# Row sums sent round by DMA, and V's high and low halves in one stationary tile, in a gated first layer followed by two attentions and a feed-forward part

## The reference

```python
def attention(x, ctx, Wq, Wk, Wv, Wo, bo):
    q, k, v = ...                                    # split in 16 heads of 64
    sim = jnp.einsum('bihd,bjhd->bhij', q, k) * SCALE
    attn = jax.nn.softmax(sim, axis=-1)
    out = jnp.einsum('bhij,bjhd->bihd', attn, v).reshape(b, n, HEADS * D_HEAD)
    return out @ Wo + bo
h = layernorm(x, ln1_g, ln1_b)
x = attention(h, h, a1_Wq, a1_Wk, a1_Wv, a1_Wo, a1_bo) + x          # 256 keys
h = layernorm(x, ln2_g, ln2_b)
x = attention(h, context, a2_Wq, a2_Wk, a2_Wv, a2_Wo, a2_bo) + x    # 120 keys
h = layernorm(x, ln3_g, ln3_b)
u, gate = jnp.split(h @ ff_Wp + ff_bp, 2, axis=-1)
x = u * jax.nn.gelu(gate, approximate=False) @ ff_Wo + ff_bo + x
```

## Time and profile before

| what | value |
|---|---|
| median of three executions (lowest, highest) | 1032.53 us (1032.07, 1035.41) |
| profiled execution: own time, span | 1037.63 us, 1035.8 us |
| TensorE matmuls busy | 997.8 us, 96% |
| VectorE busy | 709.0 us, 68% |
| ScalarE busy | 623.9 us, 60% |
| GpSimd busy | 365.7 us, 35% (16 memsets of V's zero columns: 2.4) |
| mean granted TensorE clock | 0.990 |
| chain of work that ended last | PE 81%, DVE 9%, ACT 7%, issue 2%, POOL 1% |

### The profile page before, as it was taken

The page is one execution under the profiler, slowest core; times in us unless marked ns, Lnnn a source line. Parts: engine busy times, 40 slices in busy tenths (PEclk is TensorE's granted clock), DMA queues, the critical chain, the costliest instruction groups (busy, mean ns, idle before and its releaser), DMA issues.

```text
span 1035.8 us, 21731 instructions
## 1 busy us (share of the span) xinstructions
PE 997.8 (96%) x8044; PEld 938.7 (91%) x8044; DVE 709.0 (68%) x1594; ACT 623.9 (60%) x1945; POOL 365.7 (35%) x515
## 2 busy tenths in 40 slices
PE   9899998999999999999999999999999998899998
PEld 9788777899999999999999989999999997899998
DVE  3476868867676767676768776677677667567674
ACT  2566646856565656565667666676676676434343
POOL 1021445533333333333333245455455454401010
PEclk9999999999999999999999989999999998999999
DMA  6220200103000000000003000300000001000110
GB/s 206 81 72 1 77 21 31 32 2 102 2 22 1 22 1 22 2 21 2 22 1 87 22 26 2 107 26 26 3 26 27 2 22 62 22 22 27 36 32 21
DMA packets 30446, 34.63 MB, mean 33 GB/s; under 512 B 4360, under 2 KB 23816, under 8 KB 30344
## 3 DMA queue, kind: packets, MB, share of 16 engines
q1 hardware_dynamic: 30344, 33.26, 10.5%
HBM read 24.86 MB, written 8.39 MB: 32 GB/s over the span
## 4 chain that ended last, share of the span: by engine, by line
PE 81%; DVE 9%; ACT 7%; issue 2%; POOL 1%; DVEq 0%; POOLq 0%
PE bank L1388 14%; PE bank L1390 14%; PE bank L1389 14%; PE bank L1650 8%; PE bank L1629 5%; PE bank L1412 5%; PE bank L1692 3%; PE bank L1694 3%; PE bank L1693 3%; PE bank L1666 3%; ACT p L771 2%; PE bank L1396 1%; PE bank L1519 1%; PE bank L1520 1%; PE bank L1521 1%
## 5 line engine op out<-in xcount | busy, mean ns | idle before, releaser
L578 POOL TENSOR_TENSOR oT_hi<-oT,ones 128x256 fp32r<-128x256 f32 x128 | 93.9, 733 | 364.2 <-DVE oT L1184 364.2
L771 ACT ACTIVATE p<-bank,negmax 128x256 f32<-128x256 f32 (+1 forms) x512 | 207.7, 427 | 20.8 <-DVE negmax L1161 16.0
L781 ACT CAST pT_hi<-bank 128x512 fp32r<-128x512 f32 (+1 forms) x256 | 110.8, 486 | 164.6 <-PE bank L1650 164.4
L1388 PE MATMUL bank<-hT_hi,w_hi 128*128 128x256 f32 x640 | 188.4, 294 | 4.9 <-DVE qkT_lo L1215 1.6
L1390 PE MATMUL bank<-hT_hi,w_lo 128*128 128x256 f32 x640 | 179.2, 280 | 0.0
L1389 PE MATMUL bank<-hT_lo,w_hi 128*128 128x256 f32 x640 | 179.0, 280 | 0.0
L1176 DVE TENSOR_TENSOR pT_lo<-bank,pT_hi 128x512 fp32r<-128x512 f32 (+1 forms) x256 | 129.6, 548 | 0.4
L1388 PEld LDWEIGHTS bank<-hT_hi,w_hi 128*128 128x128 f32 x640 | 121.6, 190 | 8.2 <-issue 4.7
L1157 DVE TENSOR_REDUCE negmax<-bank 128x2 f32<-128x512 f32 x128 | 82.2, 684 | 66.9 <-PE bank L1629 66.9
L1389 PEld LDWEIGHTS bank<-hT_lo,w_hi 128*128 128x128 f32 x640 | 121.3, 189 | 0.0
L1390 PEld LDWEIGHTS bank<-hT_hi,w_lo 128*128 128x128 f32 x640 | 120.9, 189 | 0.0
(11 more groups left out here) (207 smaller groups left out, 2773.4 us busy)
## 6 DMA issues: line engine op xcount, KB each, us to landing
w_stage<-in_weights SPq DMA_DIRECT2D x47, 256.0 KB, 4.0
x_in<-x_dram SPq DMA_DIRECT2D x24, 256.0 KB, 2.9
x_dram<-x_out SPq DMA_DIRECT2D x16, 256.0 KB, 3.2
l_x<-in_x SPq DMA_DIRECT2D x4, 512.0 KB, 5.3
x_dram<-l_out SPq DMA_DIRECT2D x4, 512.0 KB, 2.8
out_dram<-x_out SPq DMA_DIRECT2D x8, 256.0 KB, 3.2
w_stage<-in_weights SPq DMA_DIRECT2D x9, 128.0 KB, 4.4
l_ctx<-in_ctx SPq DMA_DIRECT2D x4, 180.0 KB, 4.6
```

Of the source, the lines that this page charges most:

```text
L578: nc.gpsimd.tensor_tensor(oh[:, G % PAIRS, :], of[:, :], ones[:, :], ALU.mult).then_inc(y["o_hi"], 1)
L771: last = nc.scalar.activation(p[:, G % 2, e, t * cols:(t + 1) * cols], scores_at(G, e, t), ACT.Exp, bias=negmax[:, G % 2, t, e:e + 1], acc ...
L781: nc.scalar.copy(pTh[0:r, G % 2, e, 0:n], bank[4 + e][0:r, 0:n]).then_inc(y["pT_hi"], 1)
L1388: nc.tensor.matmul(dst, lh, rh, start=(i == 0), stop=False)
```

## The change

The widened and transposed row sums are gone. The reciprocals of a pair go by DMA: `send_sums` writes them to DRAM as two rows of 256, one for each head, and `spread_sums` reads each row back to 64 partitions of `rsumT`, which has four buffers (`DEEP`). GpSimd multiplies, in `split_o`. V has one tile, in which each head has 128 columns, high and low side by side, and both halves of the transposed exponentials are multiplied by all 128. So low x low is summed too. The low values of a head come out on the other 64 partitions; ScalarE copies them across and VectorE adds. In cross-attention the head products alternate between banks 6 and 2, the scores between 0 and 1, and the transposed exponentials of both heads of a pair share one bank (4 or 5 in turn), with one copy and one subtraction for a pair. SP's list becomes a loop over the 128 steps with the loads, stores and weight units placed in it.

```diff
-VW = 3 * DH
+VW = 2 * DH
+DEEP = 4
...
+            def send_sums(G):
+                sp.wait_ge(y["rsum"], G + 1)
+                if G >= DEEP:
+                    sp.wait_ge(*spread_until(G - DEEP))
+                sp.dma_start(sums_dram[G % DEEP, :, :].rearrange("e (q t) -> q e t", t=NT),
+                             rs[:, G % 2, :].rearrange("q (e t) -> q e t", e=2)).then_inc(y[f"rsum_row{G % 2}"], 16)
+            def spread_sums(G):
+                sp.wait_ge(y[f"rsum_row{G % 2}"], 16 * (G // 2 + 1))
+                if G >= 2:
+                    sp.wait_ge(*spread_until(G - 2))
+                if G >= DEEP:
+                    sp.wait_ge(y["o_norm"], G - DEEP + 1)
+                for e in range(2):
+                    sp.dma_start(rT[e * DH:(e + 1) * DH, G % DEEP, :],
+                                 sums_dram[G % DEEP, e:e + 1, :].partition_broadcast(DH)).then_inc(y[f"rT{G % 2}"], 16)
...
-            for b in range(3 * B):
-                if b + 3 < 3 * B:
-                    load(b + 3)
-                store(b)
...
+            for G in range(STEPS):
+                b, i = divmod(G, PAIRS)
+                send_sums(G)
+                if G >= 1:
+                    spread_sums(G - 1)
...
+                if i == 3 and b >= 1:
+                    store(b - 1)
+                if i == 4:
+                    load(b + 2)
+                if i == 5 and B < b + 2 < 2 * B:
+                    load_context(b + 2)
+                if b == 1 and i < 4:
+                    load_weights(sp, 12 + i, 13 + i)
...
+                if b == 2 * B - 1 and i >= 6:
+                    load_weights(sp, 18 + i, 19 + i)
...
-            def widen_sums(G):
...
             def split_o(G):
+                pool.wait_ge(y["o_sum"], G + 1)
+                pool.wait_ge(*spread_until(G))
...
+                nc.gpsimd.tensor_tensor(on[:, :].rearrange("p (t q) -> p t q", t=NT),
+                                        of[:, G % DEEP, :].rearrange("p (t q) -> p t q", t=NT),
+                                        rT[:, G % DEEP, :].rearrange("p (q t) -> p t q", t=NT),
+                                        ALU.mult).then_inc(y["o_norm"], 1)
...
-            def copy_rT(G):
+            def copy_low_values(G):
                 act.wait_ge(y["o"], G + 1)
-                nc.scalar.copy(rT[:, :], bank[6][:, S:2 * S]).then_inc(y["rT_copied"], 1)
+                if G >= 2:
+                    act.wait_ge(y["o_sum"], G - 1)
+                nc.scalar.copy(ob[0:DH, G % 2, :], o_bank(G)[DH:128, 0:S])
+                nc.scalar.copy(ob[DH:128, G % 2, :], o_bank(G)[0:DH, S:2 * S]).then_inc(y["o_low"], 1)
...
             def inverse_sums(G):
                 dve.wait_ge(y["exp"], 2 * G + 2)
+                if G >= 2:
+                    dve.wait_ge(y[f"rsum_row{G % 2}"], 16 * (G // 2))
...
-            def normalise_o(G):
+            def add_low_values(G):
+                dve.wait_ge(y["o_low"], G + 1)
+                if G >= DEEP:
+                    dve.wait_ge(y["o_norm"], G - DEEP + 1)
+                nc.vector.tensor_tensor(of[0:DH, G % DEEP, :], o_bank(G)[0:DH, 0:S], ob[0:DH, G % 2, :], ALU.add)
+                nc.vector.tensor_tensor(of[DH:128, G % DEEP, :], o_bank(G)[DH:128, S:2 * S], ob[DH:128, G % 2, :],
+                                        ALU.add).then_inc(y["o_sum"], 1)
...
             def transpose_p(G):
...
+                else:
+                    pe.wait_ge(y["pT_lo"], 2 * G - 1 if G == STEPS // 2 else 2 * G - 2)
+                    for e in range(2):
+                        pe.wait_ge(y["exp"], 2 * G + e + 1)
+                        for t in range(NT):
+                            last = nc.tensor.transpose(pT_both(G)[:, e, t * 128:(t + 1) * 128],
+                                                       p[:, G % 2, e, t * SC:(t + 1) * SC], ident[:, :])
+                    last.then_inc(y["pT"], 2)
             def weighted_values(G):
...
+                    pe.wait_ge(y["o_sum"], G if G < STEPS // 2 else G - 1)
...
+                for e in range(2):
+                    dst = o_bank(G)[:, e * S:(e + 1) * S]
+                    for j in range(tiles):
+                        vs = vv[0:r, j, (2 * g + e) * VW:(2 * g + e + 1) * VW]
+                        pc = slice(j * S, (j + 1) * S)
+                        nc.tensor.matmul(dst, vs, pTh[0:r, G % 2, e, pc], start=(j == 0), stop=False)
+                        last = nc.tensor.matmul(dst, vs, pTl[0:r, G % 2, e, pc], start=False, stop=(j == tiles - 1))
```

More of the change, by code:

```diff
@@ L280, in build, with spread_until @@
         LAST = NI - 1
+        sums_dram = nc.dram_tensor("rsums_dram", (DEEP, 2, S), F32, kind="Internal").ap()
+        def spread_until(G):
+            return y[f"rT{G % 2}"], 32 * (G // 2 + 1)
         def out_banks(it):
@@ L338, in v_src, with v_dst @@
             return v_bank(b, c)[0:v_rows(b), :].rearrange("p (g e d) -> p g e d", g=4, e=2)
-        def v_dst(buf, b, c):
-            half = slice(c % 2 * 4 * VW, (c % 2 + 1) * 4 * VW)
-            return buf[0:v_rows(b), c // 2, half].rearrange("p (g s d) -> p g s d", g=4, s=3)[:, :, 0:3:2, :]
+        def v_dst(b, c, low):
+            part = vv[0:v_rows(b), c // 2, c % 2 * 4 * 2 * VW:(c % 2 + 1) * 4 * 2 * VW]
+            part = part.rearrange("p (g s d) -> p g s d", g=4, s=4)
+            return part[:, :, 1:3, :] if low else part[:, :, 0:4:3, :]
         def first_c():
@@ L380, in score_bank, with o_bank, pT_both @@
         def score_bank(G, e):
-            return bank[(2 * G + e) % 3 if G < STEPS // 2 else G % 3]
+            return bank[(2 * G + e) % 3 if G < STEPS // 2 else G % 2]
+        def o_bank(G):
+            return bank[6 if G < STEPS // 2 or G % 2 else 2]
+        def pT_both(G):
+            return bank[4 + G % 2][0:SC, :].rearrange("p (e n) -> p e n", e=2)
         def scores_at(G, e, t):
@@ L545, in first_layer @@
                     add_bias(0)
-                    pool.wait_ge(z["rps"], KT * NI)
-                    for v_ in (vh, vl):
-                        for pr in range(PAIRS):
-                            last = nc.gpsimd.memset(v_[:, :, pr * VW + DH:pr * VW + 2 * DH].bitcast(F32), 0.0)
-                    last.then_inc(zeros_ready, 1)
                 if it >= 1:
@@ L1174, in pT_low @@
[L1174 to L1184 removed]
+                if cols_of(G) == S:
+                    for e in range(2):
+                        dve.wait_ge(y["pT_hi"], 2 * G + e + 1)
+                        nc.vector.tensor_tensor(pTl[:, G % 2, e, :], bank[4 + e][:, :],
+                                                pTh[:, G % 2, e, :].bitcast(F32),
+                                                ALU.subtract).then_inc(y["pT_lo"], 1)
+                else:
+                    dve.wait_ge(y["pT_hi"], 2 * G + 2)
+                    nc.vector.tensor_tensor(pTl[0:SC, G % 2, :, 0:S], pT_both(G),
+                                            pTh[0:SC, G % 2, :, 0:S].bitcast(F32),
+                                            ALU.subtract).then_inc(y["pT_lo"], 2)
```

148 lines of the change are left out of this document (65 added, 83 removed).

## The result

The changed kernel takes 1043.14 us (median of six runs, 1038.82 to 1044.64) against 1033.97 for the kernel before on the same chip: a ratio of 1.0066, 95% interval 1.0034 to 1.0098. I had forecast 999. The profiled execution took 1038.82 us, its span is 1037.0.

| stage | before | after | change | forecast | full width | upper half first | short chain |
|---|---|---|---|---|---|---|---|
| self-attention | 412.3 | 381.9 | -30.4 | -38 | 375.0 | 378.6 | 383.9 |
| cross-attention to step 127 | 296.4 | 324.2 | +27.8 | -4 + 8.6 | 294.1 | 311.9 | 287.9 |
| from step 127 on | 153.0 | 157.0 | +4.0 | 0 | 156.6 | 155.9 | 157.2 |

The account below looks back on a forecast made before the run. TensorE was taken to bound self-attention, a VectorE and ScalarE hand-over chain cross-attention. From 1032.5 us: -38 self-attention, -4 cross-attention, +8.6 clock falls, sum -33.4, giving 999 us; range 976 to 1015.

Parts of the forecast that it names:

- -38: Self-attention: TensorE stays the bound and loses transposes and products, six middle batches 32.4 us, first 3.5, last 2.
- -4 + 8.6: Cross-attention: 4 us saved by the batches, 8.6 us lost to two new falls of TensorE's clock.
- a chain that TensorE's savings don't shorten: Cross-attention: batches run on VectorE and ScalarE handing over to each other; a middle batch saves 0.6 us, not 4.9.
- rival 4: Row sums' DMA round trip limits the steps, from landings of 5.2 us on; slower than before, 1100 us at 6.0; chance 0.04.
- rival 5: VectorE becomes the bound in self-attention too, half of the 38 us stays away: 1018 us; chance 0.06.
- Rival 1: TensorE is the bound in cross-attention too, the chain has slack: 957 us, or 973 for half; chance 0.16.
- A second one started right behind the first adds less than its duration: Split copy and addition per pair: second instruction overlaps the first, adding 0.33 us on VectorE and 0.27 on ScalarE.
- 4.2 and 5.1: Cross-attention from i = 2 on: distances in us between successive maxima on VectorE, today 3.87 and 4.77.
- The clock: Cross-attention: a 2.8 us TensorE wait at i = 4 brings two falls to 1.2 GHz, 4.3 us each, +8.6.
- rival 3: Cross-attention: the clock falls in six or seven batches, +28 us instead of +8.6, 1018 us; chance 0.10.
- 0 to +2: Start of the feed-forward part: last pair's output about 1.3 us later, last weight units loaded late; taken as 0.
- 3.6 + 1: Cross-attention savings in us: 3.6 from six middle batches, about 1 from the first; the last 0.

Follow-up runs that it names:

- full width: Changed kernel with one 128-partition copy and one addition per pair instead of two each of 64, crossing of the halves left out: 1001.68 us, ratio 0.9674.
- upper half first: Changed kernel with its two additions swapped, partitions 64 to 127 before 0 to 63: 1027.01 us, ratio 0.9917.
- short chain: Changed kernel, cross-attention reordered: context at i = 3, maxima first, additions deferred, hidden state's low half at i = 4; last two weight loads earlier: 1001.97 us, ratio 0.9665.
- the twins: Kernel before plus one unread 64-partition instruction each on ScalarE and VectorE per pair, starting at partition 0 (1048.45 us) or 64 (1081.04 us).

## Why the prediction was wrong

**Right.** Self-attention stays TensorE's stage: middle batches of 46.40 us against 46.1, and 46.10 with the upper half first. The places of the waits in cross-attention were right too: at i = 1 for the key halves (0.5 us, forecast 0.3 to 0.4) and for GpSimd (0.4, forecast 0.6), and ahead of the key products at i = 4. One of 0.8 us for the normalised hidden state was not among my three. Right was also "a chain that TensorE's savings don't shorten". The DMAs cost next to nothing (rival 4), and VectorE wasn't the bound of middle batches in self-attention (rival 5). Rival 1, TensorE as the bound, was never near. TensorE's shorter waits in the batch at 641.92 (us in total, times, longest):

```profile
PE bank L1665 <- DVE xhat L1185: 0.8, 1, 0.8
PE bank L1446 <- DVE qkT_lo L1267: 0.5, 1, 0.5
PE bank L1755 <- POOL oT_lo L621: 0.4, 1, 0.4
```

**The step that failed** is "A second one started right behind the first adds less than its duration [...] I take +0.33 us on VectorE and +0.27 on ScalarE for each pair". Measured 0.66 and 0.50. The price came from two instructions of 128 partitions in a row, both starting at partition 0. The halves start at 0 and at 64, and the row for that case stood in the same trace: two of 64x480 took 1.33 us at 0.653 each, no overlap at all. I used that row for the duration and not for the distance, and I looked at no instruction behind the halves, though the hold reaches two further.

It carried through three sizes:
- First and last batch of self-attention: -0.1 and +0.6 us instead of -3.5 and -2, the six in between -30.9 instead of -32.4. With full width the first and the last are 3.3 and 1.2 us below before. The last batch also has weights to convert in both kernels.
- Distances between maxima in cross-attention: 4.54 and 5.60 us instead of 4.2 and 5.1; TensorE's wait 3.16 (3.44 from start to start, where the seven lie between 2.9 and 4.6) instead of 2.8. By the run that fills the wait, the chain alone costs cross-attention 11.6 us where I had it gain 4.
- **The clock**, the second step that failed: I counted two new falls, +8.6; it fell in every batch (rival 3, to which I gave 0.10). Filling the wait gives back 19 us, 16 of them in cross-attention. My two reasons were one row that held, whose wait was 1.45 us, and one that fell; with a forecast wait of 2.8 us that recurs identically in each batch, one or two falls was not a consistent case: what happens in one such batch is to be expected in all, and so it was in the twins, in no middle batch of one and in each of the other. Rival 3 alone would still have ended faster than before, at 1018, since it had the halves at the low price. It took both errors to reach 1043: without the halves the kernel takes 1001.7 us, with them and the wait filled 1023.9, both below the kernel before.

**The sum.** Self-attention 7.6 us short, cross-attention 23.2, the last stage 4.0 (there the output projection waits 2.12 us for GpSimd's low half and the clock falls once more, and I had taken 0 of "0 to +2"), less 0.2 in the first stage: 34.6. The other 9.4 between 999 and 1043 are the profiled executions: before, it stood 5.1 above the median that I used; after, 4.3 below. In my own sum for cross-attention 3.6 + 1 make 4.6, which I had put in as 4.

**What stays open**: how the last stage's loss divides between its wait, the clock and the DMAs, and what decides between waits of 2.3 to 2.7 us that lower the clock and those that don't.

## What to carry to other kernels

Price an added instruction by the distance between starts in a row that has its start partitions, not by duration or by a row of like size; and look at the two instructions behind it. Where halves can't be avoided, put the one last that starts where the next instruction starts. Where a hand-over chain of two engines sets a batch, an added 0.1 us counts as often as the chain runs through it, and if the waiting engine's wait recurs unchanged, count the fall of the clock in every turn or in none; before an optimisation of TensorE's work in such a stage, reorder the chain, and fill a wait that can't be removed.

## What the hardware showed that I had not expected

- A change of start partition between neighbours costs VectorE 0.10 to 0.13 us for each instruction that it holds, up to three in a row here, and ScalarE 0.11 to 0.12. Over 128 pairs, with what the clock added, the twin runs lie 33 us apart.
- 28 useless transposes in each of seven batches made the kernel 19 us faster.
- A DMA of 256 pieces of 8 bytes lands in 3.3 us, no slower than one of 256 KB (3.7 for `x_dram`; medians of one trace).
